# Scores ahead of P times V in phases 1 to 3, with scans, jobs and tail placed anew

## What is computed

```python
x = _layernorm(x + attn(x))          # 16 heads of 32, q, k, v each times Wdown, softmax, P V, times Wup, Wo
x = _layernorm(x + xattn(x, ctx))    # per head: r = decay * r + ctx*ctx over time; out = x * r
x = _layernorm(x + ffn(x))           # silu(x Wg') * (x Wu') , times Wd'; 512 -> 2048 -> 512
# Wg, Wu, Wd are cubic splines of a few thousand control points each
```

## Time and profile before

| | |
|---|---|
| median of 3 runs | 684.98 us (684.93 to 685.54) |
| profiled run | 685.51 us, its span 683.7 us |
| PE busy | 656.8 us (96%) |
| DVE busy | 449.5 us (66%) |
| ACT busy | 347.7 us (51%) |
| POOL busy | 294.3 us (43%) |

### The profile page before, as it was taken

The page is one execution under the profiler, slowest core; times in us unless marked ns, Lnnn a source line. Parts: engine busy times, 40 slices in busy tenths (PEclk is TensorE's granted clock), DMA queues, the critical chain, the costliest instruction groups (busy, mean ns, idle before and its releaser), DMA issues.

```text
span 683.7 us, 12025 instructions
## 1 busy us (share of the span) xinstructions
PE 656.8 (96%) x4312; PEld 533.8 (78%) x4312; DVE 449.5 (66%) x826; ACT 347.7 (51%) x1002; POOL 294.3 (43%) x351
## 2 busy tenths in 40 slices
PE   9999999999999999999988799999999999999993
PEld 9597887878888788788865577888888888888883
DVE  3567687698686877878778688666544555354434
ACT  5566546637466565656667556552334233333230
POOL 1764486886638767594674836100100001000103
PEclk9999999999999999999999999999999999999997
DMA  9621020030220311121112672741193317340301
GB/s 329 221 80 62 1 87 7 2 125 1 94 62 2 133 52 32 63 72 41 40 65 47 159 173 72 210 105 40 35 239 78 81 32 198 72 101 0 124 1 61
DMA packets 22010, 58.06 MB, mean 85 GB/s; under 512 B 4032, under 2 KB 7232, under 8 KB 21056
## 3 DMA queue, kind: packets, MB, share of 16 engines
q1 hardware_dynamic: 16720, 44.45, 22.5%
q0 software_dynamic: 4944, 12.32, 5.9%
q10 hardware_dynamic: 288, 0.52, 0.2%
HBM read 32.11 MB, written 8.39 MB: 59 GB/s over the span
## 4 chain that ended last, share of the span: by engine, by line
PE 78%; DVE 12%; ACT 6%; issue 2%; POOL 1%; DVEq 0%; POOLq 0%; ACTq 0%
PE bank L303 19%; PE bank L305 18%; PE bank L304 18%; PE bank L490 6%; ACT probs L665 5%; PE bank L478 4%; DVE recurrence_T L896 4%; PE bank L512 4%; DVE minus_max L821 3%; PE bank L1191 2%; PE bank L1096 2%; DVE probsT L835 2%; PE bank L529 1%; PE bank L316 1%; PE bank L498 1%
## 5 line engine op out<-in xcount | busy, mean ns | idle before, releaser
L665 ACT ACTIVATE probs<-bank,minus_max 128x256 f32<-128x256 f32 x256 | 117.3, 486 | 23.8 <-DVE minus_max L821 23.8
L303 PE MATMUL bank<-down,hidden_hi_lo 128*128 128x512 f32 x256 | 100.7, 393 | 1.5 <-DVE hidden_hi_lo L1402 1.5
L305 PE MATMUL bank<-down,hidden_hi_lo 128*128 128x512 f32 x256 | 100.5, 392 | 0.0
L304 PE MATMUL bank<-down,hidden_hi_lo 128*128 128x512 f32 x256 | 100.0, 391 | 0.0
L821 DVE TENSOR_REDUCE minus_max<-bank 128x2 f32<-128x512 f32 x128 | 79.3, 681 | 16.3 <-PE bank L478 16.3
L1398 DVE TENSOR_TENSOR hidden<-bank,silu 128x512 f32<-128x512 f32 x64 | 44.1, 689 | 60.9 <-PE bank L305 58.9
L1356 ACT ACTIVATE silu<-bank 128x512 f32<-128x512 f32 x64 | 38.3, 598 | 82.2 <-PE bank L305 81.3
L1402 DVE TENSOR_TENSOR hidden_hi_lo<-hidden,hidden_hi_lo 128x512 fp32r<-128x512 f32 x64 | 45.5, 711 | 40.9 <-ACT hidden_hi_lo L1369 40.8
L490 PE MATMUL bank<-ident,probs 128*128 128x128 f32 x512 | 65.5, 275 | 6.2 <-ACT probs L665 5.9
L1476 POOL TENSOR_TENSOR ffn_var_eps<-ffn_mean_var,constants 128x4 f32<-128x4 f32 x3 | 0.6, 196 | 156.5 <-DVE ffn_mean_var L1418 156.5
L490 PEld LDWEIGHTS bank<-ident,probs 128*128 128x128 f32 x512 | 56.6, 141 | 14.2 <-ACT probs L665 12.0
(11 more groups left out here) (170 smaller groups left out, 1610.8 us busy)
## 6 DMA issues: line engine op xcount, KB each, us to landing
features_by_group<-features_by_cell SPq DMA_DIRECT2D x128, 128.0 KB, 2.4
ctx_squared_T<-in_ctxT SPq DMA_DIRECT2D x8, 512.0 KB, 3.3
xres<-in_x SPq DMA_DIRECT2D x8, 512.0 KB, 4.6
x_in<-x SPq DMA_DIRECT2D x16, 256.0 KB, 3.1
x_residual<-x POOLq DMA_DIRECT2D x4, 1024.0 KB, 8.1
out_x<-x_residual POOLq DMA_DIRECT2D x16, 256.0 KB, 2.8
xin_T<-in_xT SPq DMA_DIRECT2D x7, 512.0 KB, 3.9
x<-x_rows SPq DMA_DIRECT2D x7, 512.0 KB, 4.1
```

The costliest lines, as they stand in the source:

```text
L303: nc.tensor.matmul(out, wh, xh, start=first, stop=False)
L304: nc.tensor.matmul(out, wh, xl, start=False, stop=False)
L305: return nc.tensor.matmul(out, wl, xh, start=False, stop=last)
L665: inc(nc.scalar.activation(probs[:, g, t, :], S[g][:, t * T:(t + 1) * T], ACT.Exp, bias=nmax[:, g, t:t + 1], accum_out=rsum[:, t, g:g + 1] ...
```

## The change

- `pe_batch`: in phases 1 to 3 `pe_s` of a phase stands before `pe_pv` of the phase before. DVE's `dve_max` and `dve_y` change places likewise, and ACT's `act_yh` of the phase before moves into `act_exp`, ahead of the fourth head.
- `dve_batch`: the four scans move from behind `dve_heads` of phase 2 to ahead of `dve_inverse` of phase 2. In the last batch the scans leave; `dve_size` moves from phase 3 to ahead of the inverse of phase 2; two x2 low parts (`dve_x2l`) move from phase 2 to phase 3. In batch 0 one of four low parts of Wo moves behind the maxima.
- Between the halves: one job more ahead (20 in all), the last batch's scans and recurrence transposes later.
- FFN block 0: jobs shift in step 0; batch 7's stats and size come one step later.
- Tail: DVE's last four outputs become ACT instructions of scale and bias, POOL makes the bias, SP issues the four DMAs.

```diff
@@ pe_batch
         pe_extra(pe, b, 0)
+
+        pe_s(pe, b, 1)
         if b == 0:
             pe_fold_o(pe, 3)
         pe_pv(pe, b, 0)
-
-        pe_s(pe, b, 1)
...
         pe_extra(pe, b, 1)
+
+        pe_s(pe, b, 2)
         pe_pv(pe, b, 1)
-
-        pe_s(pe, b, 2)
...
@@ act_exp
         for g in range(HG):
+            if m and g == HG - 1:
+                act_yh(act, b, m - 1)
@@ dve_batch
         if b == 0:
-            for m in range(MT):
+            for m in range(MT - 1):
                 dve_weight_lo(dve, "o", m)
+        dve_max(dve, b, 1)
+        if b == 0:
+            dve_weight_lo(dve, "o", MT - 1)
         dve_y(dve, b, 0)
-        dve_max(dve, b, 1)
...
+        dve_max(dve, b, 2)
         dve_y(dve, b, 1)
-        dve_max(dve, b, 2)
         dve_extra(dve, b, 1)
-        if not proj:
-            dve_scan(dve, b, range(2))
+        if proj:
+            dve_scan(dve, b)
+        else:
+            dve_size(dve, b - 1)
         dve_inverse(dve, b, 2)
         dve_heads(dve, b, 2)
-        if proj:
-            dve_scan(dve, b, range(KT))
-        else:
+
+        dve_max(dve, b, 3)
+        dve_y(dve, b, 2)
+        if not proj:
             dve_x2l(dve, 0, 0, B_)
             dve_x2l(dve, 0, 1, C_)
-
-        dve_y(dve, b, 2)
-        dve_max(dve, b, 3)
         dve_extra(dve, b, 2)
-        if post:
+        if post and proj:
             dve_size(dve, b - 1)
-        if not proj:
-            dve_scan(dve, b, range(2, KT))
@@
-    AHEAD_JOBS = 2 * NG + 3
+    AHEAD_JOBS = 2 * NG + 4
@@ job_of
-        i = AHEAD_JOBS + (2 * JT * g - 2 + k if g else k)
-        return i if n == 0 and i < NJOB and (g or k < 2) else None
+        i = AHEAD_JOBS + (2 * JT * g - 3 + k if g else k)
+        return i if n == 0 and i < NJOB and (g or k < 1) else None
@@ dve_step
-            if g == 0:
+            if g == 1:
                 dve_stats(dve, B - 1, 0)
-            elif g == 2:
+            elif g == 3:
                 dve_size(dve, B - 1)
-            elif g == 3:
+            elif g == 4:
                 dve_stats(dve, B - 1, 1)
@@ tensor, between the halves
-            pe_rs(pe, B - 1, 0)
-            pe_rs(pe, B - 1, 1)
...
             pe_job(pe, 2 * NG + 2, X)
+            pe_rs(pe, B - 1, 0)
+            pe_rs(pe, B - 1, 1)
+            pe.wait_ge(s["ws"], 2 * NG + 3)
+            pe_job(pe, 2 * NG + 3, X)
@@ vector, between the halves
             dve_job(dve, 2 * NG, X)
+            dve_scan(dve, B - 1)
             dve_r1(dve, B - 1, 0)
             dve_job(dve, 2 * NG + 1, X)
+            dve_stats(dve, B - 2, 1)
             dve_r1(dve, B - 1, 1)
             dve_job(dve, 2 * NG + 2, X)
+            dve_job(dve, 2 * NG + 3, X)
@@ scalar, tail
+            for t in range(BT):
+                act.wait_ge(s["nm"], t + 1)
+                inc(nc.scalar.activation(res[:, t, :], res[:, t, :], ACT.Identity, bias=fnm[:, t:t + 1], scale=frstd[:, t:t + 1]), "yout")
@@ gpsimd
             pool_norm2(pool, B - 2)
             pool_makers_out(pool, 2)
+            pool_makers_out(pool, 3)
             pool_norm1(pool, B - 1)
             pool_times(pool, B - 1)
-            pool_makers_out(pool, 3)
...
+                pool.wait_ge(s["rstd"], NB + t)
+                inc(nc.gpsimd.tensor_scalar(fnm[:, t:t + 1], fmv[:, t, 0:1], frstd[:, t:t + 1], -1.0, ALU.mult, ALU.mult), "nm")
@@ sync, tail
+            for t in range(BT):
+                sp.wait_ge(s["yout"], BT * (NB - 1) + t + 1)
+                inc(sp.dma_start(out_v[:, BT * (NB - 1) + t, :], res[:, t, :]), "last", 16)
```

More of the change, by code:

```diff
@@ L212, in program @@
     fst6, fmv = sb("ffn_bn_stats", [P, BT, 6]), sb("ffn_mean_var", [P, BT, 2])
-    fve, frstd = sb("ffn_var_eps", [P, BT]), sb("ffn_rstd", [P, BT])
+    fve, frstd, fnm = (sb(n, [P, BT]) for n in ("ffn_var_eps", "ffn_rstd", "ffn_minus_mean"))
     early, late = ExitStack(), ExitStack()
@@ L279, in program @@
              "fres xt fxh fxl f fh fl w wa ws wh wl wld "
-             "g u silu hm hh hl hused d add bn mv ve rstd yout out moments").split()
+             "g u silu hm hh hl hused d add bn mv ve rstd yout out moments nm last").split()
     s = {n: sem(f"s_{n}") for n in names}
@@ L710, in act_batch @@
         act_extra(act, b, 0)
-        act_yh(act, b, 0)
         act_exp(act, b, 1)
@@ L720, in act_batch @@
         act_extra(act, b, 1)
-        act_yh(act, b, 1)
         act_exp(act, b, 2)
@@ L735, in act_batch @@
         act_extra(act, b, 2)
-        act_yh(act, b, 2)
         act_exp(act, b, 3)
@@ L888, in dve_batch, with dve_scan @@
             dve_extra(dve, b, 3)
-    def dve_scan(dve, b, part):
-        if 0 in part:
-            dve.wait_ge(s["csq"], 2 * b + 2)
-            wait(dve, "rs", 2 * b)
-        for k in part:
+    def dve_scan(dve, b):
+        dve.wait_ge(s["csq"], 2 * b + 2)
+        wait(dve, "rs", 2 * b)
+        for k in range(KT):
             inc(nc.vector.tensor_tensor_scan(rsT[:, k, :], dec[:, k:k + 1].to_broadcast([P, T]),
@@ L1254, in pe_down @@
             if n == 0:
-                pe.wait_ge(s["wld"], 2 * JT * g + 1)
+                wait(pe, "wld", 2 * JT * g)
+                pe.wait_ge(s["wl"], AHEAD_JOBS)
         if g == 0 and n == 0:
@@ L1374, in act_step @@
         act_turn(act, n, g, 0)
-        act_fill(act, n, g, 0)
-        act_fill_hi(act, n, g, 0)
         if before(n, g):
+            act_fill(act, n, g, 0)
+            act_fill_hi(act, n, g, 0)
             act_fill(act, n, g, 1)
@@ L1381, in act_step @@
             act_silu(act, n, g, 1)
+            act_fill(act, n, g, 2)
+            act_hh(act, n, g, 1)
         else:
             act_silu(act, n, g, 1)
-            act_fill(act, n, g, 1)
-            act_fill_hi(act, n, g, 1)
-        act_fill(act, n, g, 2)
-        act_hh(act, n, g, 1)
+            act_hh(act, n, g, 1)
+            act_fill(act, n, g, 0)
+            act_fill_hi(act, n, g, 0)
         act_fill_hi(act, n, g, 2)
@@ L1420, in dve_out @@
     def dve_out(dve, n, t):
-        if n < NB - 1:
-            dve.wait_ge(s["rstd"], n + 1)
-        else:
-            wait(dve, "rstd", NB + t)
+        dve.wait_ge(s["rstd"], n + 1)
         o = res[:, t, :]
@@ L1434, in dve_step @@
         dve_turn(dve, n, g, 0)
-        dve_fill(dve, n, g, 0)
-        if ends:
-            dve_add(dve, n - 1, 1)
-        dve_fill_lo(dve, n, g, 0)
         if before(n, g):
+            dve_fill(dve, n, g, 0)
+            if ends:
+                dve_add(dve, n - 1, 1)
+            dve_fill_lo(dve, n, g, 0)
             dve_fill(dve, n, g, 1)
@@ L1549, in _ @@
                 act_batch(act, b)
-            act_fh(act, 0, 0, B_)
-            act_fh(act, 0, 1, C_)
-            act_rs1(act, B - 1)
-            act_fh(act, 0, 2, A_)
-            act_fh(act, 0, 3, B_)
+            for q, out in enumerate((B_, C_, A_, B_)):
+                act_fh(act, 0, q, out)
             act_job_hi(act, 2 * NG - 1)
@@ L1558, in _ @@
                 act_job_hi(act, i)
+                if i == AHEAD_JOBS - 2:
+                    act_rs1(act, B - 1)
             for n in range(NB):
@@ L1640, in _ @@
                 inc(nc.gpsimd.tensor_tensor(frstd[:, t:t + 1], fve[:, t:t + 1], half[:, 2, 0:1], ALU.pow), "rstd")
-            for t in range(BT):
-                pool_out(pool, NB - 1, t)
-            pool.wait_ge(s["out"], 16 * BT * NB)
+                pool.wait_ge(s["rstd"], NB + t)
+                inc(nc.gpsimd.tensor_scalar(fnm[:, t:t + 1], fmv[:, t, 0:1], frstd[:, t:t + 1], -1.0, ALU.mult, ALU.mult), "nm")
+            pool.wait_ge(s["out"], 16 * BT * (NB - 1))
         @block.sync
@@ L1691, in _ @@
                         sp_features(sp, n, g, c)
+            for t in range(BT):
+                sp.wait_ge(s["yout"], BT * (NB - 1) + t + 1)
+                inc(sp.dma_start(out_v[:, BT * (NB - 1) + t, :], res[:, t, :]), "last", 16)
+            sp.wait_ge(s["last"], 16 * BT)
     late.close()
```

29 lines of the change are left out of this document (12 added, 17 removed).

## The result

Median of 6 runs 687.91 us (686.69 to 689.62), the kernel before beside it 685.26 us (684.93 to 685.74). The ratio is 1.0041, 95% interval 1.0030 to 1.0053: the change makes the kernel 2.65 us slower. The direction was forecast, the size was not: 7.5 us were forecast, and 687.91 lies near the lower end of the range.

What follows compares the result with a forecast made beforehand. TensorE, busy 96% of the span, was taken as the bound. Terms of -0.9 + 3.85 + 1.3 + 5.6 - 2.3 = +7.55 us on the median gave 692.5 us, 1.1% slower, range 687.0 to 698.5.

Steps and rivals of the forecast that it cites:

- Change 1: Batches 0 to 6: earlier scores and scans in phase 2 fill phase 3's holes; 0.9 us gained net.
- The 4.5 us for batches 1 to 3: Phase 2 of these batches: scans beside POOL work delay the next scores 1.5 us each; 4.5 us lost.
- scans hidden everywhere: Batches 1 to 3: POOL's late start leaves DVE the port there too; 4.5 us less, 688.0 us; chance 0.10.
- the margin of 2.4 against 2.3: Phase 2, batches 4 to 6: scans take 2.4 us against 2.3 us of DVE room before the inverse; no loss.
- Change 2: Last batch: size waits for POOL's product ahead of the inverse; scores 3.7 us late, y of phase 3 3.85 late.
- Change 3: From y of the last batch to the first down product: added and later work loses 1.3 us more.
- Change 4: FFN block 0: later statistics delay POOL's makers behind norm2, and PE waits before job 40; 5.6 us lost.
- the wait ahead of job 36: FFN block 0: makers for group 5 get behind size and land about when job 36 asks; 0.2 us lost.
- the 1.0 for the statistics: FFN block 0: DVE stops 1.6 us before step 2's first hidden product, of which PE loses 1.0 us.
- Change 5: Tail: outputs move to ACT and their issue to SP, so the last output lands earlier; 2.3 us gained.
- the change does not act: Batches: scores wait for the probsT copies anyway, so phase 3 keeps its holes; 699.6 us; chance 0.03.
- Faster: Last batch and FFN: POOL's times(6) and norm2(7) are ready in time, removing both waits; 682.5 us; chance 0.09.

Runs made afterwards that it cites:

- e7: Changed kernel with last batch's size back in phase 3, batch 7's FFN statistics and size back, Wo's low parts before batch 0's maxima, fourth Wo piece before scores; 676.03 us.
- e1: Changed kernel with the size reduction of the last batch back in phase 3; 681.95 us.
- e14: Changed kernel with one POOL line moved: the copy of makers for group 6 ahead of norm2 of batch 7; 682.45 us.
- e10: e7 with only the first statistics of batch 7 one step later, at the end of step 1 of FFN block 0; 675.63 us.
- e4: Kernel before with one unused tile of 16 bytes a partition added; 682.85 us.
- e12: Kernel before with the unused tile, scores ahead of P times V, and scans of batches 0 to 6 in phase 2; 678.63 us.
- e11: e7 with batch 6's scans behind y in phase 3, plus the edits of e9 and e10; 673.84 us.
- e15: Kernel before with tile, new score order, scans moved (batch 6's in phase 3 behind y), Wo's low parts first, and new tail; 673.16 us.
- e9: e7 with the last batch's two x2 residues ahead of the maxima of phase 3; 674.36 us.

## Why the prediction was wrong in size and right in direction

**Change 1 is the step that failed**: 0.9 forecast, 4.2 measured alone. Its pieces:
- The 4.5 us for batches 1 to 3 are not there: the three were to lose 1.2 in all and gained 4.9. The 4.5 came from scans at 4.5 us, the price of scans beside POOL's products. In phase 2 POOL has y's residue and xT pieces, and the four took 3.29: the nearer row would have been the 2.42 of the earlier trace rows. PE's own work covers that; only 0.3 us reach it (phase 2 is 10.95 against 10.66 for phase 1). The rival "scans hidden everywhere" was true of this place.
- Phases 1 and 2 of batches 1 to 3 became shorter too, from 11.07 to 10.66 and 10.95. The prediction counted holes in phase 3 alone.
- In batches 4 to 6 the scans took 3.42 us and not the 2.4 of the prediction, and batches 4 and 5 lost nothing by it. That they were free there was right, the margin of 2.4 against 2.3 was not.
- In batch 0 the wait for the fourth low part was forecast (Q at 35.2, measured 34.79) and priced at 1.2; e7 gives 1.06 for it. What was missing is the half clock behind it, 1.5 more in some executions.
- Phase 2 of batch 6 was taken to be free, by its likeness to batches 4 and 5. It lost 2.2 us in the trace. The likeness fails in one item of POOL's queue.

**Change 2 was right**: DVE stops 5.19 us, the scores of phase 3 are 3.4 late (3.7 forecast) and y 4.30 (3.85 forecast), with half clock in the last part. Undone alone it gives 5.96. By the profiled runs 4.5 of it is this stretch; e1's batches 0 to 6 are also 1.15 us earlier, without half clock in batch 0, and its FFN is 1.0 longer.

**Change 3**: 0.80 for 1.3, within its ends.

**Change 4 was right in mechanism**: issue of the makers 438.56 (437.9), hole 3.5 (4.4), and e14 shows that it is POOL's queue. The half clock behind it, 1.7, was missing, and the wait ahead of job 36 was 0.97 where 0.2 was forecast; the 1.0 for the statistics was too high, since by e10 their place is worth 0.4 or nothing. Measured 4.13 for the stretch, but 1.7 to 2.0 of gain by the tile's address lie in it (208.94 us from the last job to the last gate product before, 207.24 after, 206.97 in e4). Against e4's 276.45 for the whole stretch the term is 6.3. That this is near 5.6 is luck: two terms too high and two too low.

**Change 5 was mis-sized**: 2.3 forecast, 3.6 measured. (The recorded times 680.4 and 682.5 differ by 2.1, not 2.3.) The prediction kept 2.8 us of landing for the last DMA; SP's land in 2.0, and the span ends 2.1 us behind the last issue and not 3.8. The last issue starts 1.2 us behind the last rstd (within 1 forecast).

**Not in the sum at all**: the address, 2.25 us gained by a tile that the diff shows as one word. Nothing in the trace of before could have priced it; its gate and up products at 390 to 397 ns beside 390 to 392 for the down products were the only sign.

Against 7.55, on the two profiled runs: -3.6 (change 1), +0.45 (2), -0.5 (3), -1.5 (4, the address within), -1.3 (5) leave 1.17. The medians differ by 2.65, since after's median is 1.2 above its profiled run and before's 0.25 below. The executions of after differ by up to 2.9 us (before: 0.8), with granted clocks from 0.983 to 0.989: it has more holes, and the profiles show that not all of them are followed by half clock in each execution.

The rival "the change does not act" is refuted by e12. "Faster" named the two waits and priced them at 10.0 together; its condition (POOL in time) did not come true, but with both taken out the kernel is 9.2 faster at 678.73, 0.98% under before, and with the waits of batches 0 and 6 mended as well 674.1. What stays open is what 6.83 us at half clock cost in the last batch, and whether the last batch of e11 with the FFN of e15 would be faster than either.

## What to carry to other kernels

Before an instruction is moved on an engine that waits for another, write down what stands ahead of the awaited one in that engine's queue; here a copy that did not need the layer norm stood behind it, and one line was worth 5.5 us. Cost a moved instruction at the row whose neighbours on the shared port are those of the new place, batch by batch, and look for the one batch whose queue differs. When a change adds a tile, time the old kernel with that tile alone, or its effect is laid to the wrong part. When two runs differ by some 1.5 us, look first whether one has a stretch at half clock that the other lacks; the profiled differences of e7 and e9 have such a part.

## What the runs showed of the hardware that was not expected

- Addresses: most of the same float32 gate and up matmuls stand 229 to 236 ns apart before, and 226 to 227 with every tile behind one place 32 bytes later; 2.25 us of 685. Only this one shift (from 32 above a multiple of 64 to a multiple of 64) was tried, so whether 64 is what counts is not shown. The coefficients did not move; which of the other operands does it was not separated.
- Half clock behind a hole of PE: behind holes of 1.0 to 5.0 us the granted clock was 0.50 for 3.41 or 6.83 us in some executions and not in others. For 3.41 us it cost 1.5 to 1.7 us where PE had no slack (batch 0, batch 6, job 40) and 0.9 to 1.0 in the last batch, where PE has holes.
- A copy of 0.42 us took 3.14, and four scans of 2.42 took 5.55, beside POOL's products.
